# A gather of 32 samples by 4 fields in place of 4 samples by 32, with the squares scaled on ScalarE

## What is computed

```
gathered = emb[f, xi[b, f]]                # 2048 x 32 rows of 496
e  = gathered * xv[:, :, None]
s  = sum over fields of e
qi = 0.5 * (s * s - sum over fields of e * e)
h  = relu(xv @ W1 + b1)                    # 32 -> 1024
y  = concatenate([qi, h]) @ W2 + b2        # one number for each sample
```

## Time and profile before

| | us |
|---|---|
| median of 3 runs (lowest, highest) | 659.15 (658.28, 659.45) |
| profiled execution | 656.74 |
| its span | 654.9 |
| POOL busy | 485.8 (74%) |
| DVE busy | 384.4 (59%) |
| PE busy | 308.0 (47%) |
| ACT busy | 265.8 (41%) |

### The profile page before, as it was taken

How to read it: one execution, slowest core, us unless ns; L and a number is a source line. 1 busy time by engine, 2 the same in 40 slices (tenths; PEclk the granted TensorE clock), 3 DMA queues, 4 the chain that set the end, 5 groups by cost and what they waited for, 6 DMA issues and landing times.

```text
span 654.9 us, 4973 instructions
## 1 busy us (share of the span) xinstructions
PE 308.0 (47%) x1122; PEld 55.9 (9%) x1122; DVE 384.4 (59%) x1330; ACT 265.8 (41%) x273; POOL 485.8 (74%) x521
## 2 busy tenths in 40 slices
PE   1544536354453643546346353453635445364354
PEld 0101001010010100101001010100101001010010
DVE  6556655656666465655556555665555665556554
ACT  2344444434443434344343434444344444343433
POOL 5777777777777777777777777777777777777773
DMA  7777777777777777777777777777777777777774
GB/s 218 203 205 203 203 205 204 203 203 203 203 204 204 203 204 202 207 201 204 204 203 205 204 203 203 203 206 204 203 204 202 204 203 205 205 203 202 204 202 114
DMA packets 33647, 132.08 MB, mean 202 GB/s; under 512 B 8577, under 2 KB 8721, under 8 KB 33586
## 3 DMA queue, kind: packets, MB, share of 16 engines
q0 software_dynamic: 32768, 130.06, 72.4%
q1 hardware_dynamic: 752, 1.31, 0.7%
q10 hardware_dynamic: 98, 0.40, 0.2%
HBM read 131.72 MB, written 0.01 MB: 201 GB/s over the span
## 4 chain that ended last, share of the span: by engine, by line
POOL 60%; issue 20%; PE 10%; DMA 8%; DVE 1%; POOLq 0%; ACT 0%; DVEq 0%
POOL gathered L142 60%; DMA gathered<-emb,index_rows 7%; PE sum_ps L189 6%; PE hidden_ps L202 5%; DMA index_raw<-index 0%; POOLq L139 0%; DVE weighted L271 0%; POOLq L33 0%; ACT squares L160 0%; DVE weighted L300 0%; PE norm_ps L209 0%; DVE index_rows L227 0%; DVE y_rows L310 0%; DVE index_wrap L224 0%; DVE norms_scaled L288 0%
## 5 line engine op out<-in xcount | busy, mean ns | idle before, releaser
L142 POOL DMA_INDIRECT gathered<-emb,index_rows x512 | 484.8, 947 | 158.8 <-issue 151.1
L271 DVE SCALAR_TENSOR_TENSOR weighted<-squares,w_all 128x496 f32<-128x496 f32 x512 | 324.6, 672 | 261.3 <-ACT squares L160 261.0
L160 ACT ACTIVATE squares<-gathered 128x992 f32<-128x992 f32 x256 | 256.3, 1001 | 366.2 <-DMA gathered<-emb,index_rows 343.1
L189 PE MATMUL sum_ps<-gathered,weights 128*32 128x496 f32 x1024 | 240.8, 1031 | 343.4 <-DMA gathered<-emb,index_rows 343.4
L189 PEld LDWEIGHTS sum_ps<-gathered,weights 128*32 128x32 f32 x1024 | 29.0, 140 | 526.8 <-issue 526.8
L202 PE MATMUL hidden_ps<-w_b,value_rows 33*128 33x512 f32 x64 | 60.5, 1097 | 0.0
L271 DVE DVE_READ_ACCUMULATOR weighted<-squares,w_all 128x1 f32 x512 | 42.4, 83 | 0.0
L202 PEld LDWEIGHTS hidden_ps<-w_b,value_rows 33*128 33x128 f32 x64 | 18.6, 321 | 42.4 <-issue 42.4
L283 DVE SCALAR_TENSOR_TENSOR weighted<-hidden_ps,w_all 128x512 f32<-128x512 f32 x32 | 20.7, 686 | 0.0
L166 ACT ACTIVATE sum_squared<-sum_ps 128x496 f32<-128x496 f32 x16 | 9.3, 583 | 16.8 <-PE sum_ps L189 16.8
L233 DVE TENSOR_TENSOR weights<-values,own_row 128x16 f32<-128x16 f32 x128 | 12.7, 170 | 0.0
(11 more groups left out here) (19 smaller groups left out, 7.3 us busy)
## 6 DMA issues: line engine op xcount, KB each, us to landing
gathered<-emb,index_rows POOLq DMA_INDIRECT x512, 3.7
w_all<-w SPq DMA_DIRECT2D x1, 760.0 KB, 6.1
values<-value SPq DMA_DIRECT2D x1, 256.0 KB, 3.5
value_rows<-value_t ACTq DMA_DIRECT2D x1, 256.0 KB
index_raw<-index SPq DMA_DIRECT2D x1, 240.0 KB, 4.7
w_b<-w ACTq DMA_DIRECT2D x1, 128.0 KB
index_raw<-index SPq DMA_DIRECT2D x1, 16.0 KB, 3.0
w_b<-b ACTq DMA_DIRECT2D x1, 4.0 KB
```

Of the source, the lines that this page charges most:

```text
L142: nc.gpsimd.indirect_dma_start(out=gathered[:, s, j, :], out_offset=None, in_=emb, in_offset=bass.IndirectOffsetOnAxis(ap=index_rows[:, g: ...
L160: nc.scalar.activation(squares[:, pair, 0:dim], gathered[:, s, pair], ACT.Square).then_inc(squared, 1)
L189: last = nc.tensor.matmul(sum_ps[j * COLS:(j + 1) * COLS, 0:dim], weights[:, i % 2, s, j, :], gathered[:, s, j, :], start=(s == 0), stop=( ...
L271: nc.vector.scalar_tensor_tensor(weighted[:, j, 0:dim], squares[:, j, 0:dim], -0.5, w2_all[:, 0:dim], ALU.mult, ALU.mult, accum_out=norms[ ...
```

## The change

A gather now holds 32 samples by 4 fields. A block is 4 turns `t` of 8 gathers: 4 groups of 32 samples (`j`), and for each a pair (`k`) of gathers with four fields each. So every partition of a pair belongs to one sample, and the parts of its sum need not be told apart before the end.

ACT squares gather by gather and gives the sample's value for the field as a scale that is read per partition, so that the square is already value squared times row squared. DVE weighs the two gathers of a pair in one instruction of 992 elements. The products of value squared (L288) and the spreading (L293) go. The sums over partitions of norms, hidden layer and squared sums are made once, at the end of the program, by three matmuls. PE does 8 matmuls for each turn and waits for ACT's squares of the whole turn (in the last turn of all for the gathers themselves). POOL waits for PE once in 8 gathers. The matrices of `weights` have 32 columns, all filled by one DVE instruction for each block that multiplies the values by a mask held in PSUM. The weighing of the squared sums moves from the end of a block to the end of the next block's first turn (`weigh_sums`), and ACT's squaring of the sums moves there too.

```
         @block.gpsimd
             for i in range(blocks):
...
+                for t in range(turns):
                     if i > 0:
-                        pool.wait_ge(squared, ((i - 1) * quads + s + 1) * pairs)
-                        pool.wait_ge(summed, (i - 1) * quads + s + 1)
+                        pool.wait_ge(summed, (i - 1) * turns + t + 1)
                     for j in range(GROUPS):
+                        for k in range(pair):
+                            g = i * in_block + (t * GROUPS + j) * pair + k
+                            nc.gpsimd.indirect_dma_start(
+                                out=gathered[:, t, j, k, :], out_offset=None, in_=emb,
+                                in_offset=bass.IndirectOffsetOnAxis(ap=index_rows[:, g:g + 1], axis=0),
+                            ).then_inc(fetched[t][j], 16)

         @block.scalar
+            def square_sums(i):
+                act.wait_ge(summed, (i + 1) * turns)
                 if i > 0:
                     act.wait_ge(sum_squared_used, i)
+                nc.scalar.activation(sum_squared[:], sum_ps[:, 0:dim],
                                      ACT.Square).then_inc(sum_squared_ready, 1)
...
+                for t in range(turns):
+                    for j in range(GROUPS):
+                        if j % 2 == 0 and i + t + j > 0:
+                            act.wait_ge(normed, (i * turns + t) * GROUPS // 2 + j // 2)
+                        act.wait_ge(fetched[t][j], (i + 1) * pair_arrived)
+                        for k in range(pair):
+                            g = i * in_block + (t * GROUPS + j) * pair + k
+                            last = nc.scalar.activation(
+                                squares[:, j % 2, k, 0:dim], gathered[:, t, j, k], ACT.Square,
+                                scale=values[:, g:g + 1])
+                        last.then_inc(squared, 1)
+                    if t == 0 and i > 0:
+                        square_sums(i - 1)
+            square_sums(blocks - 1)

         @block.tensor
+                for t in range(turns):
+                    if i == blocks - 1 and t == turns - 1:
+                        for j in range(GROUPS):
+                            pe.wait_ge(fetched[t][j], (i + 1) * pair_arrived)
+                    else:
+                        pe.wait_ge(squared, (i * turns + t + 1) * GROUPS)
+                    if t == 0 and i > 0:
                         pe.wait_ge(sum_squared_ready, i)
+                    for k in range(pair):
+                        for j in range(GROUPS):
+                            last = nc.tensor.matmul(sum_ps[j * COLS:(j + 1) * COLS, 0:dim],
+                                                    weights[:, i % 2, (t * GROUPS + j) * pair + k, :],
+                                                    gathered[:, t, j, k, :], ...)
                     last.then_inc(summed, 1)
+                    if t == 1:
...                                            # the hidden layer's two matmuls, as before
+            pe.wait_ge(hidden_lines_ready, 1)
+            add_lines(hidden_lines, True, False)
+            pe.wait_ge(norm_lines_ready, 1)
+            add_lines(norm_lines, False, False)
+            pe.wait_ge(sum_lines_ready, 1)
+            add_lines(sum_lines, False, True).then_inc(y_summed, 1)

         @block.vector
+            def refill_weights(i):
+                nc.vector.scalar_tensor_tensor(
+                    weights[:, i % 2],
+                    values[:, i * in_block:(i + 1) * in_block].unsqueeze(2).to_broadcast(
+                        [P, in_block, COLS]), 1.0,
+                    y_ps[:, P:P + COLS].unsqueeze(1).to_broadcast([P, in_block, COLS]),
+                    ALU.mult, ALU.mult).then_inc(weights_ready, 1)
+            def weigh_sums(i):
+                dve.wait_ge(sum_squared_ready, i + 1)
+                nc.vector.scalar_tensor_tensor(
+                    weighted_sums[:], sum_squared[:], 0.5, w2_all[:, 0:dim], ALU.mult, ALU.mult,
+                    accum_out=sum_part[:, i:i + 1]).then_inc(sum_squared_used, 1)
...
+                for t in range(turns):
+                    for j in range(GROUPS):
+                        dve.wait_ge(squared, (i * turns + t) * GROUPS + j + 1)
+                        last = nc.vector.scalar_tensor_tensor(
+                            weighted[:, j % 2], squares[:, j % 2, :, 0:dim], -0.5,
+                            w2_all[:, 0:dim].unsqueeze(1).to_broadcast([P, pair, dim]),
+                            ALU.mult, ALU.mult, accum_out=norms[:, i, t, j:j + 1])
+                        if j % 2 == 1:
+                            last.then_inc(normed, 1)
+                    if t == 0 and i > 0:
+                        weigh_sums(i - 1)
+                    if t == 1 and i + 1 < blocks:
+                        if i > 0:
+                            dve.wait_ge(summed, i * turns)
+                        refill_weights(i + 1)
+                    if t == 2:
+                        dve.wait_ge(hidden_ready, i + 1)
...                                            # the hidden layer weighed in one instruction
+            dve.wait_ge(normed, blocks * turns * 2)
+            add_turns(blocks - 1, blocks).then_inc(norm_lines_ready, 1)
+            weigh_sums(blocks - 1)
+            dve.wait_ge(sum_squared_used, blocks)
+            by_line(sum_part, sum_lines, blocks - 1, blocks).then_inc(sum_lines_ready, 1)
+            dve.wait_ge(y_summed, 1)
+            nc.vector.tensor_scalar(y[:], y_ps[0:lines, 0:COLS], b2_all[0:lines, :], None, ALU.add
+                                    ).then_inc(y_ready, 1)
```

More of the change, by code:

```diff
@@ L22, in fm_kernel @@
     hidden = w1.shape[1]
-    per = P // fields
+    per = P // COLS
     blocks = batch // P
-    quads = P // (GROUPS * per)
+    pair = 2
+    turns = fields // (per * pair)
     gathers = index.shape[1]
-    in_block = quads * GROUPS
+    in_block = turns * GROUPS * pair
     halves = hidden // 512
-    pairs = 2
-    pair_arrived = 16 * GROUPS // pairs
-    assert per * quads == COLS and gathers == blocks * in_block and dim <= 512
+    pair_arrived = 16 * pair
+    lines = blocks * GROUPS
+    assert per * pair * turns == fields and gathers == blocks * in_block and dim <= 512
+    assert lines <= P and halves == 2
     with ExitStack() as ctx:
@@ L45, in fm_kernel @@
         index_rows = sb("index_rows", [P, gathers], I32)
[L46 to L55, removed]
+        values = sb("values", [P, gathers])
@@ L56, in fm_kernel @@
         w2_all = sb("w2_all", [P, dim + hidden])
+        b2_all = sb("b2_all", [P, 1])
         w1_b1 = sb("w1_b1", [fields + 1, hidden])
         value_rows = sb("value_rows", [fields + 1, batch])
[L59 to L72, removed]
+        sum_squared = sb("sum_squared", [P, dim])
+        norms = sb("norms", [P, blocks, turns, GROUPS])
+        norm_lines = sb("norm_lines", [P, blocks, GROUPS])
+        hidden_part = sb("hidden_part", [P, blocks])
+        sum_part = sb("sum_part", [P, blocks])
@@ L205, in _, with add_lines @@
                         last.then_inc(hidden_ready, 1)
-            sum_norms(blocks - 1)
-            pe.wait_ge(identity_ready, 1)
-            pe.wait_ge(y_ready, blocks)
-            nc.tensor.matmul(norm_ps[0:blocks, P:2 * P], y[:], identity[:], start=True, stop=True
-                             ).then_inc(y_turned, 1)
+            def add_lines(part, first, last):
+                return nc.tensor.matmul(y_ps[0:lines, 0:COLS], part[:].rearrange("p i j -> p (i j)"),
+                                        own_sample[:], start=first, stop=last)
+            pe.wait_ge(hidden_lines_ready, 1)
[4 more added lines that the diff above has]
+            add_lines(sum_lines, False, True).then_inc(y_summed, 1)
         @block.vector
@@ L244, in _ @@
             dve.wait_ge(rows_known, per)
-            step(nc.vector.tensor_scalar(last_row[:], first_row[:], float(vocab - 1), None, ALU.add))
             dve.wait_ge(first_loaded, 16)
-            rows_of(slice(0, in_block))
-            nc.vector.memset(weights[:], 0.0)
-            nc.vector.memset(ones[:], 1.0)
-            step(nc.vector.memset(own_row[:], 0.0))
-            for b in range(per):
-                last = nc.vector.memset(own_row[b * fields:(b + 1) * fields, b:b + 1], 1.0)
@@ L257, in _ @@
             dve.wait_ge(index_loaded, 16)
-            rows_of(slice(in_block, gathers))
-            dve.wait_ge(rows_known, per + 1)
-            nc.vector.tensor_scalar(identity[:], column_less_row[:], 0.0, None, ALU.is_equal
-                                    ).then_inc(identity_ready, 1)
+            rows_of(1, blocks)
+            step(nc.vector.memset(own_group[:], 0.0))
+            for j in range(GROUPS):
+                last = nc.vector.memset(own_group[j * COLS:(j + 1) * COLS, j:j + 1], 1.0)
@@ L262, in _ @@
+            step(last)
             dve.wait_ge(w1_loaded, 48)
```

194 lines of the change are left out of this document (77 added, 117 removed).

## The result

The changed kernel takes 663.58 us (median of 4 runs, 662.67 to 664.64) where the kernel before takes 658.80 (four runs) beside it: a ratio of 1.0073, 95% interval 1.0059 to 1.0087. It is slower, by 4.8 us. The forecast was 664.7. On the chip of a later set both were a little quicker, with about the same distance (5.3 us): 662.03 against 656.74, ratio 1.0082 [1.0068, 1.0096]. In two of the four later sets of runs (e0 to e3 and e7 to e9), each on another chip, gathers landed late for part of the time, also in the kernel before, which took 754 us there: from those I read single gathers, and the sums from a1, e4, e5, e6 and e10.

A forecast was written before the change was run, and what follows sets the result against it. POOL issuing gathers, one every 1.25 us, was taken as the bound. Terms 4.6 - 0.3 - 0.1 + 1.4 = +5.6 took the profiled 656.74 to 662.3, and 2.4 for the runs' median gave 664.7 us; range 659.5 to 667.5.

The forecast's parts named there:

- Gathers and waits of POOL, no change: POOL's loop: still 512 gathers at 1.25 us each; fewer waits for PE win nothing, as they cost nothing before.
- The rule read from the rows: A gather starting while a VectorE instruction with two SBUF inputs runs loses what is left of it less about 0.13 us.
- ACT, DVE and PE lie beside POOL: Ordinary work on the other engines is hidden beside POOL; ACT 309 us in all, DVE's main weighing 284 for 307.
- The losses removed, -0.3: Main loop: removing L288, L293, L305, L241 and the norm matmul ends four later POOL losses, -0.3 us.
- `weigh_sums` over POOL's start, +4.6: In 15 of 16 blocks it starts 0.23 before a gather, which loses 0.31 us: +4.6 us.
- The rule of the Trainium skill on the port: Two-SBUF-input VectorE contends with GpSimd reading SBUF; the first keeps the port throughout; to the letter, 2.0 us higher.
- Start, -0.1: Setup: first gather again at 4.97, three setup losses gone (-0.35), two new losses of 0.4; -0.1 us taken.
- End, +1.4: Behind the last gather: PE's 8 matmuls instead of 4 add 1.81 us, the path behind PE loses 0.44; +1.4 us.
- The 2.4 us between the profiled execution and the runs: Kernel before: the runs' median 659.15 lies 2.4 above the profiled execution; the same difference was added to the forecast.
- A: Rival: `weigh_sums` falls clear of POOL's gather starts, leaving +1.0 us, 660.1; chance 0.20.
- B: Rival: unprofiled runs of the kernel before lose more to the old two-input instructions, so -1.4 us, 657.7; chance 0.10.
- C: Rival: equal rows in fields 12 and 27 queue, landings grow towards 5.5, end +1.8 us, 666.5; chance 0.08.

The follow-up runs named there:

- e0: The kernel before, unchanged, run once more with late landings: 753.62 us (kernel before beside it 754.00).
- e3: Changed kernel with `weigh_sums` over 992 elements, so it lasts 1.19 instead of 0.67 us: 738.05 us with late landings (kernel before 754.0).
- e7: Changed kernel with `weigh_sums` done twice in a row: 741.18 us with late landings (kernel before 754.34).
- e9: Same kernel as e2, run again: changed kernel with 0.36 us of DVE work ahead of `weigh_sums`; 736.76 us with late landings (kernel before 754.34).
- a1: The changed kernel, unchanged, run once more: 662.03 us, ratio 1.0082 to the kernel before.
- e4: Changed kernel with the squared sums left in PSUM, so `weigh_sums` reads one SBUF tensor instead of two: 656.82 us, ratio 1.0001 to the kernel before.
- e5: Kernel of e4 plus a semaphore for each of the last eight gathers, PE multiplying each as it lands: 655.14 us, ratio 0.9975 to the kernel before.
- e6: Changed kernel without ACT's per-partition scale, so its output is another: 660.14 us, ratio 1.0054 to the kernel before.
- e10: Kernel before with the tile `squares` in SBUF instead of PSUM, so its main DVE weighing reads two SBUF tensors: 717.83 us against 656.71.
- e2: Changed kernel with 0.36 us of DVE work on a PSUM tile put in front of `weigh_sums` in the loop: 733.2 us with late landings (kernel before 754.0).
- e1: Changed kernel with the squared sums left in PSUM, so `weigh_sums` reads one SBUF tensor: 739.5 us with late landings (kernel before 754.0).

## Why the prediction came out right, step by step

- **Gathers and waits of POOL, no change.** Right: a1 has a plain step of 1.2498, POOL waits for PE nowhere. The +1.5 us of the first profile's plain steps is of the execution (a1, e5).
- **The rule read from the rows.** The size (the rest less 0.13) and the order are right, but the "one thing in common" was misread. L222 reads one tensor in SBUF, `index_raw`, and writes to SBUF, and the gather under it loses the same: by its rest less 0.13 in all four profiles of the kernel before and its variant, and so does the one under L227. In the loop the rule was applied to an instruction with two SBUF inputs, where it holds.
- **ACT, DVE and PE lie beside POOL.** Right. ACT's busy time went from 265.8 to 335.4 (309 was forecast, without a price for the scale) and POOL did not notice, except through the place of `weigh_sums`. L304 reads PSUM and one SBUF tensor as L271 did: in the ten profiles of the changed kernel and its variants some 1500 gathers started well inside it and none took longer.
- **The losses removed, -0.3.** Right: the four are gone.
- **`weigh_sums` over POOL's start, +4.6.** Right in mechanism and size: 5.0 us in the profiled run, 4.8 in a1, and 5.2 us of the median come back in e4. Two terms were off and in part cancel. ACT's pair takes 1.27 and not 1.17, and ACT starts 3.76 and not 3.70 after the gather in the block shown, so the lead is 0.08 to 0.26 instead of 0.23 and a loss 0.38 on average instead of 0.31; and two or three blocks in fifteen lose nothing because the lead has shrunk below 0.04. That 13 x 0.38 comes so near 15 x 0.31 is luck. The price of the operand that the prediction quoted from the Trainium skill ("ScalarE: Activation LUTs", What ACT_TABLE_LOAD costs), 93 ns, agrees with the trace: L176 takes 668 ns with the scale and 578 without it in e6. By it the prediction had a pair of 1.27 and a loss of 0.41, nearer than my own term for a single block; the sum of 15 such losses, 6.1, would have been farther off.
- **The rule of the Trainium skill on the port** ("SBUF — State Buffer", Who interferes with whom). Who began first decides (e2), an instruction with two SBUF inputs does it and the same one with an input in PSUM doesn't (e4), and the gather is held to the instruction's end (e3). The letter of the rule would give the full rest; every run gives 0.13 less. That this is the time that a gather spends before it first needs the port is an inference that no run here tests.
- **Start, -0.1.** Wrong: -0.85 in the profile, and outside the bounds that I gave. The first gather comes 0.65 sooner, where I had it again at 4.97, and two of the three setup losses are gone (0.13 and 0.07); neither of the two new ones came. The third, 0.15, can't go with them: the first gather of the program takes 1.09 in all fourteen profiles. The first index load takes 2.6 us instead of 3.0 to land, and the two instructions behind it 0.19 each instead of 0.25 and 0.30. Why the load lands sooner was not tried.
- **End, +1.4.** Right, +1.26: PE's sixteen instructions take 3.53 (3.69 was forecast), and what follows them 4.33 (4.26).
- **The 2.4 us between the profiled execution and the runs.** Wrong: in the changed kernel the profiled execution (663.38) lies 0.2 below the median. The kernel before has a median of 656.74 in the 21 runs beside a1, which is the time of its profiled execution: the 2.4 do not belong to being profiled. So the sum of the terms was 1.1 too low for the profiled execution (662.3 for 663.38), the 2.4 on top made it 1.1 too high for the median, and the nearness of 664.7 is in part luck.
- **Rivals.** A (clear of the start) happens in two or three blocks, not in all; the lead there is 0.04 us or less. B (unprofiled runs lose more in the kernel before) is out: e4, which has no loss in the loop, is not faster than the kernel before (1.0001), its later end (some 1.3) being paid by its earlier start (some 0.7) and by the old losses that are gone (some 0.4). C (equal rows) is out: landings are 3.4 / 3.7 / 5.5 us as before.

The total was 0.8 us too high on the difference (5.6 for 4.8), and 0.3 too high against the second set (5.3). By a1's profile, whose plain steps are those of the kernel before, the 5.0 between the spans are: start -0.74, the new losses +4.83, the old ones -0.34, end +1.46, other steps -0.21.

## What to carry to other kernels

Where POOL issues gathers back to back and sets the pace, look at what VectorE reads: an instruction with two inputs in SBUF that is running when a gather starts delays it by its rest less 0.13 us, and one such instruction in a bad place cost more (5.0 us) than the three of the kernel before together (0.3). Put one of its inputs in PSUM, or see that it begins after the gather. The two setup instructions that read one tensor from SBUF and write to SBUF (L222, L227) delayed gathers in the same way; those with an input in PSUM did not. Where work recurs at a fixed distance from a landing, its place in POOL's step can be worked out to some 0.1 us before it is built, and a sum that depends on a lead of 0.1 us should be given with the chance that it vanishes.

## What was not expected of the hardware

TensorE's granted clock. In the kernel before, with landings on time, it was 1.00 throughout. Now it falls after some 80 us; by windows, the changed kernel for 28.3 to 32.0, 300 to 340 and 653.6 to 657.3 us (the clock is the third number from the end):

```profile
28.30:32.00 3.70, 3.61 (x17) 0.74 (x17) 3.42 (x4) 1.41 (x4) 2.84 (x3) 1.00 0.70 196
300.00:340.00 40.00, 17.84 (x68) 3.63 (x68) 21.83 (x36) 20.38 (x34) 30.34 (x32) 0.50 0.73 201
653.60:657.30 3.70, 3.58 (x17) 0.79 (x18) 1.51 (x5) 1.27 (x2) 0.00 (x0) 0.50 0.00 0
```

0.50 is the level of 1.2 GHz, where the kernel before has 1.00 in the same stretch. With late landings the kernel before, too, has means of 0.64 to 0.67 over a run. What PE does before it is different: it waits some 7 us between turns (7.10 before the sums at 220.55, in the timeline above), where it waited some 3 us between steps; that this is the cause was not tried. The clock cost nothing here: e4, as quick as the kernel before, has 0.54 for 300 to 340 us, and PE is nowhere on the path but at the end. At the end, too, it shows no price:

```profile
28.39 3.54 PE L201 MATMUL sum_ps<-gathered,weights 128*32 128x496 f32 x16 [6.50 <-ACT squares L176]
...
653.72 3.53 PE L201 MATMUL sum_ps<-gathered,weights 128*32 128x496 f32 x16 [5.65 <-DMA gathered<-emb,index_rows]
```

The sixteen instructions take as long at 0.50 as at 1.00. Why was not tried.

With late landings, the five variants of the changed kernel that ran there are 1.7 to 2.8% faster than the kernel before (e2: 0.9716 [0.9692, 0.9740]), though e1's edit, once landings were on time (e4), brought it level with the kernel before and no further. The changed kernel itself was not run in such a set. What makes the landings late and why this order of work bears them better was not tried and stays open.
